# Wide cross attention: keys stored without zero blocks, and the two heads of a block as two half-height score products in different PSUM banks

## The reference

```python
h, d = (16, 64)
q = (x @ Wq).reshape(b, n, h, d).transpose(0, 2, 1, 3)        # x: layer-normed, 256 wide
k = (context @ Wk).reshape(b, -1, h, d).transpose(0, 2, 1, 3)  # 154 context rows
v = (context @ Wv).reshape(b, -1, h, d).transpose(0, 2, 1, 3)
sim = jnp.einsum('bhid,bhjd->bhij', q, k) * d ** (-0.5)
attn = jax.nn.softmax(sim, axis=-1)
out = jnp.einsum('bhij,bhjd->bhid', attn, v)
return out.transpose(0, 2, 1, 3).reshape(b, n, h * d) @ Wo + bo
```

## Time and profile before

| what | us |
|---|---|
| three runs | 1631.83, 1632.54, 1640.22 |
| their median | 1632.54 |
| the profiled execution's own time | 1640.96 |
| its span | 1639.2 |
| `project_out` in it | about 329 to 370 |
| `Cross.run` in it | about 370 to 650 |

### The profile page before, as it was taken

One profiled execution on the slowest core, in us unless ns is written; L12 is line 12 of the kernel. 1 busy time (PEld: TensorE's weight loads), 2 busy tenths in 40 slices (PEclk: granted clock), 3 DMA queues, 4 the chain that ended last, 5 costly groups with the idle time before them and its releaser, 6 DMA issues. The chain is left out here.

```text
span 1639.2 us, 28274 instructions
## 1 busy us (share of the span) xinstructions
PE 1366.2 (83%) x10043; PEld 1050.4 (64%) x10043; DVE 1028.7 (63%) x2072; ACT 863.3 (53%) x2157; POOL 438.7 (27%) x594
## 2 busy tenths in 40 slices
PE   5899999996999998799966654888854699999975
PEld 3534444365999997567754424677744688888973
DVE  5788787263566654556658864666636577777743
ACT  5246667743666664311116633656631577777843
POOL 5212122281333432000005541000000244444420
PEclk9989999997999999699986766999977799999997
DMA  4825422000000000200010012111003566666734
GB/s 93 217 50 142 69 41 41 2 4 1 2 1 1 1 1 1 84 1 0 1 42 0 1 30 62 31 30 40 21 22 106 164 202 204 203 204 206 219 100 154
DMA packets 96319, 114.57 MB, mean 70 GB/s; under 512 B 23229, under 2 KB 81587, under 8 KB 96179
## 3 DMA queue, kind: packets, MB, share of 16 engines
q1 hardware_dynamic: 86115, 97.99, 22.4%
q0 software_dynamic: 4416, 12.06, 2.2%
q10 hardware_dynamic: 5648, 2.70, 0.7%
HBM read 88.74 MB, written 16.55 MB: 64 GB/s over the span
## 5 line engine op out<-in xcount | busy, mean ns | idle before, releaser
L822 ACT ACTIVATE sa_probs<-ps 128x512 f32<-128x512 f32 (+1 forms) x304 | 154.4, 578 | 86.1 <-PE ps L775 85.0
L846 DVE TENSOR_REDUCE sa_top<-ps 128x2 f32<-128x1024 f32 (+3 forms) x160 | 171.9, 1114 | 39.2 <-PE ps L751 25.3
L2239 PE MATMUL ps<-me_h,me_w_parts 128*128 128x256 f32 x1104 | 143.9, 291 | 17.9 <-issue 16.5
L2239 PEld LDWEIGHTS ps<-me_h,me_w_parts 128*128 128x128 f32 x1104 | 138.7, 195 | 22.8 <-issue 19.4
L2782 ACT ACTIVATE room<-ps,cx_top 128x154 f32<-128x154 f32 x256 | 97.2, 389 | 89.8 <-DVE cx_top L2846 89.8
L2253 PE MATMUL ps<-me_w_parts,me_mid 128*128 128x256 f32 x1104 | 136.2, 283 | 5.8 <-DVE me_result L2333 5.8
L2253 PEld LDWEIGHTS ps<-me_w_parts,me_mid 128*128 128x128 f32 x1104 | 132.3, 188 | 9.9 <-issue 9.9
L2303 ACT ACTIVATE me_full<-ps,me_b 128x256 f32<-128x256 f32 x184 | 94.9, 516 | 70.1 <-PE ps L2239 67.0
L2316 DVE TENSOR_TENSOR me_w_parts<-me_chunk,me_w_parts 128x1024 fp32r<-128x1024 f32 x92 | 117.8, 1282 | 17.7 <-ACT me_w_parts L2280 15.1
L2345 DVE TENSOR_TENSOR me_mid<-me_full,me_mid 128x256 fp32r<-128x256 f32 x184 | 84.8, 465 | 66.5 <-ACT me_mid L2305 61.6
L2644 POOL TENSOR_TENSOR room<-room,cx_rinv 128x512 f32<-128x512 f32 x64 | 66.7, 1042 | 173.7 <-DVE cx_rinv L2854 173.6
(11 more groups left out here) (421 smaller groups left out, 3420.1 us busy)
## 6 DMA issues: line engine op xcount, KB each, us to landing
me_chunk<-in_L_ffn_W_dram SPq DMA_DIRECT2D x92, 512.0 KB, 3.9
sa_k<-scr_k SPq DMA_DIRECT2D x48, 128.0 KB, 4.5
sa_q<-scr_q SPq DMA_DIRECT2D x96, 64.0 KB, 4.8
cn_qd<-cn_qh SPq DMA_DIRECT2D x64, 64.0 KB, 2.1
scr_q<-room SPq DMA_DIRECT2D x6, 512.0 KB, 5.1
scr_k<-room SPq DMA_DIRECT2D x6, 512.0 KB, 5.5
me_b<-in_L_ffn_b_dram SPq DMA_DIRECT2D x23, 128.0 KB, 4.5
x<-in_x_dram SPq DMA_DIRECT2D x4, 512.0 KB, 6.1
```

The costliest lines, as they stand in the source:

```text
L822: act.activation(probs[:, step % self.PROBS, h0:h0 + many, 0:w], src[:, :, 0:w], ACT.Exp, scale=DH ** -0.5).then_inc(exped.sem, 1)
L846: dve.tensor_reduce(top2[:, k % 2, k0 // 512, h0:h0 + many, sb % HBLK], src[:, :, 0:w], AX.X, ALU.max).then_inc(freed.sem, 1)
L2239: last = pe.matmul(ps[:, MID + n % 4, 0:RT], w[:, u % 2, 0, i, DM * k + P * b:DM * k + P * b + P], h[:, u % 2, j, k, :], start=(m == 0), s ...
```

## The change

The keys' tiles lose the axis of pieces: `kh` and `kl` are now [128, batch, block, 154], head 2m in the upper 64 partitions and head 2m+1 in the lower 64, without zeros. The two clearing instructions of GpSimd and the waits on them go, and ScalarE and VectorE write each block with one instruction over 128 partitions in place of two over 64.

The scores of a block are six products in place of three: `half_score(n, j, k)` has weights of 64 rows by 128 columns (partitions 64j to 64j+63 of the queries) and streams the 154 columns of its head's keys into columns 154j on of the bank of n. `scores(n)` issues them in pairs: the even head of step n + 1 (upper rows, bank (n+1) % 3) and the odd head of step n (lower rows, bank n % 3). So each step's even half is made one step early, ahead of the loop by `scores(-1)` for the first. Three waits follow: for `exp` n - 2 (the last user of bank (n + 1) % 3) where it was `exp` n - 3, for a new signal `s_even` that the even half of n has been completed, and for the next pair's queries one step earlier, with the second round of queries moved from s = 6 to s = 5.

```diff
-                pool.memset(cross.kh[:, :, :, :, :].bitcast(F32), 0.0).then_inc(k_zero.sem, 1)
-                pool.memset(cross.kl[:, :, :, :, :].bitcast(F32), 0.0).then_inc(k_zero.sem, 1)
...
-                    for j in range(HB):
-                        last = act.activation(cross.kh[W * j:W * j + W, :, m, j, :],
-                                              ps[W * j:W * j + W, m % 4, 0:KB].rearrange("p (b k) -> p b k", b=B), ACT.Copy)
-                    last.then_inc(k_high.sem, 1)
+                    act.activation(cross.kh[:, :, m, :], ps[:, m % 4, 0:KB].rearrange("p (b k) -> p b k", b=B), ACT.Copy
+                                   ).then_inc(k_high.sem, 1)
...
-        Q_AT = (2, 6) if wide else (3,)
+        Q_AT = (2, 5) if wide else (3,)
...
-                    for k, (a, v) in enumerate(((qh, self.kh), (ql, self.kh), (qh, self.kl))):
-                        last = pe.matmul(ps[:, S_BANK + n % SR, 0:M * hn], a[:, g % 2, m, P * i:P * i + P],
-                                         v[:, b, m, j:j + hn, :], start=(k == 0), stop=(k == 2))
-                    last.then_inc(s_s.sem, 1)
+                def half_score(n, j, k):
+                    t, m = divmod(n, NS)
+                    b, g, i = t // ST, t // PAIR, t % PAIR
+                    rows = slice(W * j, W * j + W)
+                    a, v = ((qh, self.kh), (ql, self.kh), (qh, self.kl))[k]
+                    return pe.matmul(ps[:, S_BANK + n % SR, M * j:M * j + M], a[rows, g % 2, m, P * i:P * i + P],
+                                     v[rows, b, m, :], start=(j == 0 and k == 0), stop=(j == 1 and k == 2),
+                                     skip_group_check=True)
+                def scores(n):
+                    ahead = n + 1
+                    if ahead < NS * NT:
+                        if ahead % (NS * PAIR) == 0:
+                            pe.wait_ge(s_ql.sem, s_ql.at(QR * (ahead // (NS * PAIR)) + QR))
+                        if ahead >= SR:
+                            pe.wait_ge(s_exp.sem, s_exp.at(ahead - SR + 1))
+                    if n >= 0:
+                        pe.wait_ge(s_even.sem, s_even.at(n + 1))
+                    for k in range(3):
+                        if ahead < NS * NT:
+                            even = half_score(ahead, 0, k)
+                            if k == 2:
+                                even.then_inc(s_even.sem, 1)
+                        if n >= 0:
+                            last = half_score(n, 1, k)
+                    if n >= 0:
+                        last.then_inc(s_s.sem, 1)
```

More of the change, by code:

```diff
@@ L931, in project_out @@
                                                                                "biased"))
-        r_zero, k_zero, kmm, k_high, k_low, vmm, v_set, r_set, q_high, q_low, o_high, o_low = (
-            c.sig("cp_" + k) for k in ("r_zero", "k_zero", "kmm", "k_high", "k_low", "vmm", "v_set", "r_set", "q_high",
+        r_zero, kmm, k_high, k_low, vmm, v_set, r_set, q_high, q_low, o_high, o_low = (
+            c.sig("cp_" + k) for k in ("r_zero", "kmm", "k_high", "k_low", "vmm", "v_set", "r_set", "q_high",
                                        "q_low", "o_high", "o_low"))
@@ L1057, in _ @@
                 ln.vector(dve)
-                dve.wait_ge(k_zero.sem, k_zero.at(2))
                 for m in range(MB):
                     dve.wait_ge(k_high.sem, k_high.at(m + 1))
[L1061 to L1066, removed]
+                    dve.tensor_tensor(cross.kl[:, :, m, :], ps[:, m % 4, 0:KB].rearrange("p (b k) -> p b k", b=B),
+                                      raw(cross.kh[:, :, m, :]), ALU.subtract).then_inc(k_low.sem, 1)
                     if m in (2, 4):
@@ L1078, in project_out @@
         c.rowstat.done()
-        for s, k in ((bo_in, 16), (turned, NT), (copied, NT), (mm, NT), (added, NT), (biased, NT), (r_zero, 1), (k_zero, 2),
+        for s, k in ((bo_in, 16), (turned, NT), (copied, NT), (mm, NT), (added, NT), (biased, NT), (r_zero, 1),
                      (kmm, MB), (k_high, MB), (k_low, MB), (vmm, NV + B), (v_set, NV), (r_set, 4 * B), (q_high, KD),
@@ L2558, in __init__ @@
         self.wql = sb("wql", [P, KD, H * self.width], F32R)
-        self.kh = sb("kh", [P, B, self.blocks, self.hb, M], F32R)
-        self.kl = sb("kl", [P, B, self.blocks, self.hb, M], F32R)
+        self.kh = sb("kh", [P, B, self.blocks, M], F32R)
+        self.kl = sb("kl", [P, B, self.blocks, M], F32R)
         self.vm = sb("vm", [P, B, H, self.vw])
@@ L2595, in run @@
         s_xn, s_x, s_xh, s_xl, s_q, s_qh, s_ql, s_s, s_top, s_exp, s_rinv, s_norm, s_t, s_ta, s_td, s_o, s_oh, s_ol, \
-            s_out, s_add, s_biased, s_pad = (c.sig("cr_" + k) for k in (
+            s_out, s_add, s_biased, s_pad, s_even = (c.sig("cr_" + k) for k in (
                 "xn", "x", "xh", "xl", "q", "qh", "ql", "s", "top", "exp", "rinv", "norm", "t", "ta", "td", "o", "oh",
-                "ol", "out", "add", "biased", "pad"))
+                "ol", "out", "add", "biased", "pad", "even"))
         TURNS = (0, 1, 4, 2, 3) if wide else (0, 1, 2, 3, 4)
@@ L2673, in queries @@
                     last.then_inc(s_q.sem, 1)
-                def scores(t, s):
-                    n = NS * t + s
-                    m, h, hn = groups[s]
+                def half_score(n, j, k):
+                    t, m = divmod(n, NS)
                     b, g, i = t // ST, t // PAIR, t % PAIR
[L2679 to L2683, removed]
-                    for k, (a, v) in enumerate(((qh, self.kh), (ql, self.kh), (qh, self.kl))):
-                        last = pe.matmul(ps[:, S_BANK + n % SR, 0:M * hn], a[:, g % 2, m, P * i:P * i + P],
-                                         v[:, b, m, j:j + hn, :], start=(k == 0), stop=(k == 2))
-                    last.then_inc(s_s.sem, 1)
+                    rows = slice(W * j, W * j + W)
[21 more added lines that the diff above has]
+                        last.then_inc(s_s.sem, 1)
                 def turn(t, i):
@@ L2734, in _ @@
                     queries(0, r)
+                scores(-1)
                 for t in range(-1, NT + 1):
@@ L2739, in _ @@
                         if t + 1 < NT:
-                            scores(t + 1, s)
+                            scores(NS * (t + 1) + s)
                         for g, r in round_at(t, s):
@@ L2910, in run @@
                      (s_norm, 4 * NT), (s_t, 5 * NT), (s_ta, len(ON_ACT) * NT), (s_td, len(ON_DVE) * NT), (s_o, RN * NT),
-                     (s_oh, RN * NT), (s_ol, RN * NT), (s_out, RN * NT), (s_add, NT), (s_biased, NT), (s_pad, 1)):
+                     (s_oh, RN * NT), (s_ol, RN * NT), (s_out, RN * NT), (s_add, NT), (s_biased, NT), (s_pad, 1), (s_even, NS * NT)):
             s.passed(n)
```

1 line of the change is left out of this document (removed).

## The result

The changed kernel takes 1667.25 us (median of 4 runs, 1664.62 to 1669.16) where the kernel before, run beside it, takes 1636.38 (4 runs, 1631.83 to 1641.31). The ratio is 1.0187, 95% interval 1.0145 to 1.0229: slower by 30.9 us. The forecast was +29.6 and 1662. The profiled execution after has a span of 1667.4 us, against 1639.2 before, +28.2.

What follows compares the result with a forecast made beforehand. TensorE's list was taken to bound `Cross.run` from end to end. The terms 29.7 + 10.4 - 1.5 - 4.2 - 2.7 - 2.1 gave +29.6 us, on the median of 1632.54 some 1662; own range 1648 to 1673.

Steps and rivals of the forecast that it cites:

- The price of the division: Scores groups: each way between full height and row halves costs 0.09 plus an exposed load of 0.107; +29.7 us, pairs' gain included.
- Two halves at once: Scores products: both row halves load and stream at once, a pair costing 0.109 not 0.142; -0.10 per group, -12.8 us.
- in turn: Rival, scores: the halves run one after the other; 1693 with divisions paid (chance 0.11), 1664 with them free (0.05).
- a load waits for the half's product: Rival, scores pairs: no load under its own half's product, so a pair costs 0.18; 1677 us, chance 0.05.
- The ring wait: Step 2 of each of 16 tiles: TensorE waits 0.65 mean for `exp` 0; +10.4 us, less 1.5 for the drain inside it.
- The two waits of `turn`: Steps 2 (every second tile) and 4: existing waits get covered because TensorE comes later; -4.2 us.
- `project_out`: End of `project_out`: half the instructions over `kh` and `kl`, so `rstd` starts near 367.9 in place of 369.98; -2.1 us.
- the zero that I took: Four rounds of queries after `project_out`: no gain assumed from the clock; -4.5 us if it stayed up, kept for the range.
- The tile as a whole: One full tile: dearer groups plus ring wait, less the drain inside it, `weigh`'s paid change and covered `turn` waits; +2.16 us.
- The first tile: First tile: its eight dearer groups and its wait are hidden while VectorE and ScalarE set the pace; -2.7 us.
- the forecast of the stage: `Cross.run`: the forecast's terms without that of `project_out`; +31.7 us.
- The sign: Whole kernel: the change makes it slower, chance 0.78, against same 0.15 and faster 0.07.

Runs made afterwards that it cites:

- the twins: Two kernels: the kernel before plus one 8-column product ahead of each group of scores, on 64 rows or all 128; 1674.95 and 1643.03 us.
- 64-row twin: The kernel before plus one unread 8-column product with weights of 64 rows ahead of each group of scores; 1674.95 us, ratio 1.0223.
- the ring alone: The kernel before, with the scores of step n waiting for `exp` n-2 in place of n-3; 1655.13 us, ratio 1.011.
- the highest first: VectorE takes the highest of step 0 ahead of `low_o` and `low_x`; 1662.5 us on the changed kernel, 1636.36 on the kernel before.
- 128-row twin: The kernel before plus one unread 8-column product with weights of all 128 rows ahead of each group of scores; 1643.03 us, ratio 1.0036.
- e8_one_by_one: The changed kernel with a group's three even-head products first and the three odd-head ones behind them, in place of pairs; 1669.73 us, ratio 1.0224.
- e2_touch_rows: Same run as the 64-row twin: the kernel before plus a 64-row, 8-column product ahead of each scores group; 1674.95 us, ratio 1.0223.
- e3_touch_full: Same run as the 128-row twin: the kernel before plus a 128-row, 8-column product ahead of each scores group; 1643.03 us, ratio 1.0036.
- e6_full_height: The changed kernel's order and waits, but keys with zero blocks, 128 rows in every product, and `project_out` as before; 1671.35 us, ratio 1.0236.

## Why the prediction came out near, and what failed

*The price of the division* (+29.7, the largest term) held. A group is 0.64 to 0.65 us where 0.68 was forecast, 0.22 more than before and not 0.257. Both gaps are there at every group, and the twins gave the price by itself. What was too dear are the loads behind the gaps. I had 0.107 each way. But the first pair costs 0.17 where the others cost 0.11, and the transposes take 0.66 where they took 0.60: 0.06 each way. Three pairs of 0.11, two gaps of 0.09 and two of these 0.06 make 0.63. Ahead of a full-height product with 308 columns, in the 64-row twin, the open part is the whole 0.10 (0.28 less two gaps).

*Two halves at once* held: pairs 0.11 apart, as I took from `weigh`'s column pairs. The rivals "in turn" and "a load waits for the half's product" are out. That products on different row groups run at once, as the Trainium skill says (TensorE: Matmul & The Clock Gate, Part 3, The mechanism), is what these rows show: 1 to 6 ns apart.

*The ring wait* held in place and cause. Its size was put at 0.74 and 0.57 us in the two kinds of tile, less the 0.09 of the drain inside it. Measured are 0.75 and 0.60 with the drain already taken off, 0.67 per tile, and 0.67 went when the wait was taken away. But it stands in tiles 2 to 15 only, fourteen and not sixteen: 9.4 us where the two terms (+10.4 and -1.5) gave 8.9. What the ring does in the first tile is another matter, below.

*The two waits of `turn`* (-4.2) went, as forecast: at step 4 the transposes follow the group in the usual 0.20. *`project_out`* (-2.1) gave 2.05: from ScalarE's first copy of keys to `rstd` are 13.7 us in all six kernels with the old layout and 11.67 in all four with the new. The other 0.55 of the table's -2.6 lie ahead of that, where executions of unchanged code differ by more. The queries after it ran at the lower level again (0.54 where 0.50 was), the zero that I took. VectorE's last three instructions over the keys and `rstd`, the rows that answer to the earlier trace rows:

```profile
364.93 1.39 DVE L1055 TENSOR_TENSOR cx_kl<-ps,cx_kh 128x308 fp32r<-128x308 f32 x3
367.37 0.25 DVE L2508 RECIPROCAL cx_ln_rstd<-cx_ln_sd 128x16 f32<-128x16 f32 x1 [1.05 <-ACT cx_ln_sd L2512]
```

*The tile as a whole* was forecast at +2.16 and is +2.03 in the middle of the stage, because a group is 0.03 cheaper than forecast. But the sum was made with sixteen such tiles. Thirteen brought 2.01 each, and the last two, which have no queries left to make, only 1.0 together. In the kernel before TensorE already waits in each of these two, 1.24 us for the probabilities (L2695) and 0.56 us for `low_o` (L2728); in the changed kernel these waits are 0.17 and 0.21, so most of the dearer groups pass inside them. The fifteen tiles behind the first gave 27.1 where 32.4 were in the sum.

*The first tile is the step that failed.* I put its part at -2.7: all of its eight groups and its wait hidden behind VectorE and ScalarE. For the groups that held: in both twins, whose groups are dearer too, the first tile takes 9.91 us as before. For the wait it did not: the tile takes 13.88 with the ring alone and 14.64 in the changed kernel, +4.7. TensorE's one wait for `exp` in this tile before, and then two of the changed kernel's:

```profile
398.85 0.41 PE L2685 MATMUL ps<-cx_kh,cx_qh 128*128 128x308 f32 x1 [1.86 <-ACT room L2782]
```

```profile
392.99 0.49 PE L2671 MATMUL ps<-cx_kh,cx_qh 64*128 64x154 f32 x2 [1.02 <-ACT room L2789]
...
399.51 0.34 PE L2671 MATMUL ps<-cx_kh,cx_qh 64*128 64x154 f32 x2 [1.49 <-ACT room L2789]
```

There are no outputs, transposes or weighing yet in this round, only the two rounds of queries. So most steps follow each other almost at once, and the wait for `exp` n - 2 comes three times: 1.02 at step 2, 1.49 at step 5 and 1.12 at the first step of tile 1. I had sized the ring wait at step 2 of a full tile only, and not asked what it does where nothing stands between the steps.

The waits are less than half of the +4.7, though. All of TensorE's waits in this tile come to 2.0 us before and 3.9 in the changed kernel. The rest is mostly the clock: the two rounds of queries took 1.5 and 1.4 us before and take 2.9 and 2.7 now (from 393.84 and from 400.00), at the lower level for nearly all of that time. The windows from 390 to 415 us in the kernel before, in the changed one, in the changed one with the highest first, and in the 128-row twin (granted clock in the eighth column, after POOL's):

```profile
390.00:415.00 25.00, 19.21 (x149) 17.40 (x150) 14.04 (x32) 16.94 (x68) 8.96 (x13) 0.99 0.00 1
```

```profile
390.00:415.00 25.00, 21.02 (x152) 17.55 (x152) 11.74 (x27) 14.52 (x56) 7.58 (x11) 0.73 0.01 1
```

```profile
390.00:415.00 25.00, 19.91 (x114) 16.48 (x114) 9.48 (x21) 12.70 (x47) 6.17 (x9) 0.57 0.01 1
```

```profile
390.00:415.00 25.00, 21.69 (x172) 20.04 (x172) 13.84 (x32) 17.37 (x69) 8.95 (x13) 1.00 0.01 2
```

In the kernel before the clock comes up from its lower level at 390.3 and stays up. In the changed kernel it comes up only at 396.9 and falls back twice, from 400.3 to 403.7 and from 407.1 to 410.5. It fell back in the first tiles of all six kernels that have the shorter ring (the ring alone has 0.91 in this window) and in none of the four that don't (before, the two twins, and before with the highest first). In the kernel with the highest first it is low from 394.9 until 418.8. That is where most of its missing us are: from the first highest of tile 0 to that of tile 2 are 36.2 us against the changed kernel's 33.3, although each later tile is 0.67 shorter. So the clock's fall goes with the shorter ring in all ten traces, one execution of each; what in it brings the clock down was not tried apart, and why it stayed down longest in the kernel with the fewest waits stays open.

So the forecast of the stage, +31.7, met +32.6 because two misses cancelled: 5.3 too much for the fifteen tiles, against 5.4 too little in the first one (-0.7 in the sum, +4.7 measured) and the 0.8 ahead of it. The sign, the main mechanism and the second one were right; the closeness of the total is partly luck.

## What to carry to other kernels

Dividing the array by rows to avoid multiplying zeros, with shapes like these, pays only over long stretches. A pair of half products costs a load, 0.11 us, where a full product of 308 columns cost 0.142, so three of them save 0.10, while going in and out costs some 0.32 (the group's 0.65 less three pairs); at 0.033 saved by each, an estimate is that some ten pairs in a row are needed to break even, and here three stood alone. A product issued one step ahead takes a buffer out of the ring that it writes to: look for the closest two steps of the loop, and at the start-up round too, where nothing stands between them. And before reading a close total as proof, compare the forecast with the trace stretch by stretch.

## What the runs showed of the hardware

- The two row halves work through the list independently: a product fourth in the list, on the other half, started 10 ns after the first and 0.17 us before the second (e8_one_by_one).
- A change between full height and 64 rows leaves a gap of about 0.09 us each way, and behind it a part of a weight load that nothing hides: 0.06 us ahead of half products and of transposes (the changed kernel), 0.10 ahead of a product of 308 columns. A visit by one product of 8 columns costs 0.28 us (e2_touch_rows less e3_touch_full). The gap is the same for the column halves.
- At the full clock no product with 128-column weights cost less than 0.11 us here, however few columns it streams: 8 columns 0.11 (e3_touch_full), 154 columns 0.11 on all rows (e6_full_height), and a pair of 64-row products 0.11 (the changed kernel).
